# Retention stage: scores in one pass over four PSUM banks, and a chunk's work spread over one more period

## The reference, cut to what matters

```
x = x + retention(layernorm(x))          # 8 sequences of 512 rows, 256 columns, 16 heads of 16
Q, K = rotate(xn @ WQ), rotate(xn @ WK)  # position rotation
V = xn @ WV
D[h,i,j] = gamma_h ** (i-j) for i >= j, else 0
R = einsum(einsum(Q, K) * D, V)          # per head
R = group_norm(R) * gamma + beta         # over the 16 columns of a head
y = R @ WO
```

## Time and profile before

| what | value |
|---|---|
| three runs | 2053.95, 2053.84, 2051.27 us; median 2053.84 |
| the profiled execution | 2054.74 us, its span 2053.0 us |
| mean granted TensorE clock | 0.92 of full speed |
| PE busy | 1724.3 us, 84% of the span |
| PE weight loads | 1280.7 us, 62% |
| DVE, ACT, POOL busy | 1209.3 us (59%), 667.7 us (33%), 583.1 us (28%) |
| first and last transpose of XN in retention | 1438.0 and 1753.5 us from the span's start |

### The profile page before, as it was taken

How to read it: one execution, slowest core, us unless ns; L and a number is a source line. 1 busy time by engine, 2 the same in 40 slices (tenths; PEclk the granted TensorE clock), 3 DMA queues, 4 the chain that set the end, 5 groups by cost and what they waited for, 6 DMA issues and landing times. The chain is left out here.

```text
span 2053.0 us, 33292 instructions
## 1 busy us (share of the span) xinstructions
PE 1724.3 (84%) x10092; PEld 1280.7 (62%) x10092; DVE 1209.3 (59%) x3206; ACT 667.7 (33%) x2056; POOL 583.1 (28%) x668
## 2 busy tenths in 40 slices
PE   4767766999899967267857999996899999799998
PEld 2444435777677744156756888885566666456655
DVE  5999994777677765799843221222677777422221
ACT  2545554554455424012320111111344444211111
POOL 2434432000000011787516333332344443200000
PEclk9998987999999989678865999998999999799999
DMA  6000000000000000000022324222000000000000
GB/s 184 19 13 15 15 18 11 11 11 12 13 11 12 1 9 0 6 3 21 34 95 67 93 85 110 92 86 98 27 27 26 26 26 26 1 11 20 10 20 21
DMA packets 55111, 71.08 MB, mean 35 GB/s; under 512 B 7074, under 2 KB 44898, under 8 KB 54626
## 3 DMA queue, kind: packets, MB, share of 16 engines
q1 hardware_dynamic: 37218, 40.46, 6.3%
q0 software_dynamic: 6912, 18.88, 3.6%
q10 hardware_dynamic: 10880, 10.49, 1.5%
HBM read 46.61 MB, written 23.20 MB: 34 GB/s over the span
## 5 line engine op out<-in xcount | busy, mean ns | idle before, releaser
L801 ACT ACTIVATE probs<-psS,nm 128x256 f32<-128x256 f32 x256 | 118.9, 469 | 189.5 <-DVE nm L834 189.5
L409 PE MATMUL psKV<-wkv,XT 128*128 128x512 f32 x256 | 135.8, 679 | 52.2 <-DVE acc L545 32.5
L1576 DVE COPY YE<-e_psY 128x512 f32<-128x512 f32 x40 | 27.7, 691 | 220.6 <-PE e_psY L1522 220.6
L545 DVE SCALAR_TENSOR_TENSOR acc<-psKV,G,acc 128x128 f32<-128x128 f32 x544 | 150.2, 333 | 6.7 <-ACT gated L470 6.7
L1512 PE MATMUL e_psH<-e_XT,w 128*128 128x256 f32 x640 | 147.1, 384 | 0.0
L1522 PE MATMUL e_psY<-w,e_HT 128*128 128x256 f32 x640 | 144.0, 379 | 0.0
L832 DVE TENSOR_REDUCE mx<-psS 128x2 f32<-128x512 f32 x128 | 87.9, 686 | 90.9 <-PE psS L722 90.9
L722 PE MATMUL psS<-Rec,QT 128*128 128x256 f32 (+1 forms) x512 | 133.7, 384 | 5.4 <-issue 4.5
L1482 POOL DMA_INDIRECT XE<-token_rows,held x80 | 76.0, 950 | 200.2 <-PE e_psX L1499 180.5
L1522 PEld LDWEIGHTS e_psY<-w,e_HT 128*128 128x128 f32 x640 | 121.6, 190 | 16.5
L1512 PEld LDWEIGHTS e_psH<-e_XT,w 128*128 128x128 f32 x640 | 120.6, 193 | 15.4
(11 more groups left out here) (254 smaller groups left out, 3872.0 us busy)
## 6 DMA issues: line engine op xcount, KB each, us to landing
expert_out<-YE ACTq DMA_DIRECT2D x40, 256.0 KB, 2.2
w<-in_w SPq DMA_DIRECT2D x16, 512.0 KB, 4.3
X<-in_x SPq DMA_DIRECT2D x8, 512.0 KB, 7.6
x_turned<-XT SPq DMA_DIRECT2D x32, 128.0 KB, 2.1
XS<-x_turned SPq DMA_DIRECT2D x8, 512.0 KB, 4.0
token_rows<-o_XN SPq DMA_DIRECT2D x32, 128.0 KB, 1.7
out_x<-X SPq DMA_DIRECT2D x8, 512.0 KB, 2.9
QT<-in_sel SPq DMA_DIRECT2D x2, 1024.0 KB, 11.5
```

What stands on the lines that cost most here:

```text
L409: mm = pe.matmul(psKV[v % 2][half][:, :, :], XT[:, v, c, :], wkv[:, c, half * 512:(half + 1) * 512], start=(c == 0), stop=(c == KC - 1))
L545: ins = nc.vector.scalar_tensor_tensor(acc[:, v % 2, e, :], kv, g, acc[:, v % 2, e, :], ALU.mult, ALU.add)
L801: nc.scalar.activation(probs[:, b.q % 4, hg, :], psS[b.q % 2][:, hg, :], ACT.Exp, bias=nm[:, b.q % 2, hg:hg + 1], scale=scale, accum_out=s ...
```

## The change

It changes which bank holds what, how many periods a chunk passes through, and the order in every engine's list.

**Banks.** `psS` becomes four banks, one for each 32-row group, and `scores` issues all 16 products in one pass that goes round the four groups. To make room, turned x and the V product share one bank (`psXV`; the output product goes to its V half as before), R, the new state and the turned inverses share one (`psRS`), and the variances go into the first columns of `psQK`. The sharing adds waits: `project_v` waits for the next chunk's `xt_evac` (turned x read by ACT), `inverses_turned` for `st_done` (the new state read by DVE), `to_state` for `r_read` (R read by ACT), `variances` for `rot_done` (psQK read by DVE).

**Periods.** A chunk now passes through four periods after its preparation: new (0), one (-1), two (-2), three (-3). Rows are added and their statistics taken two periods ahead (before: one), normalised and turned one period ahead, gathered three ahead. Scores are made at -1; masked half at -1 and half at -2; R, its squares, variances and inverses at -2; the inverses turned, the result and the output at -3. Keys are copied at 0 and queries at -1 (XT, QT doubled, Kr four deep).

**Copies.** `values` copies V from PSUM once; the split by even and odd heads, `values_parted`, reads that copy in SBUF one period later.

```diff
-        psT = k.ps(ctx, "n_psT", [P, 2, KC, P])
+        psXV = k.ps(ctx, "n_psXV", [P, 2, D])
         psQK = k.ps(ctx, "n_psQK", [P, 2 * D])
-        psV = k.ps(ctx, "n_psV", [P, 2 * D])[:, 0:D]
         psK = k.ps(ctx, "n_psK", [P, 2, KC, P])
-        psX = k.ps(ctx, "n_psX", [P, 2, KC, P])
-        psVar, psInv = psX[:, 0, 0, 0:H1], psX[:, 1, :, :]
-        psS = [k.ps(ctx, f"n_psS{s}", [P, KC, 2, P]) for s in range(2)]
-        psR = k.ps(ctx, "n_psR", [P, 2, KC, P])[:, 0, :, :]
+        psRS = k.ps(ctx, "n_psRS", [P, 2, KC, P])
+        psS = [k.ps(ctx, f"n_psS{r}", [P, KC, 2, P]) for r in range(4)]
+        psX, psV = psXV[:, 0, :].rearrange("p (c t) -> p c t", c=KC), psXV[:, 1, :]
+        psR, psNew = psRS[:, 0, :, :], psRS[:, 1, :, :]
+        psInv, psVar = psR, psQK[:, 0:H1]
...
+            def project_v(c):
+                pe.wait_ge(xt_evac, upto(c.g + 2))
+                pe.wait_ge(z_added, c.g + 1)
...
+            def scores(c):
+                pe.wait_ge(x_evac, c.g * 2 + 4)
+                pe.wait_ge(s_masked, c.g * 4 + 4)
+                for h in range(KC):
                     for par in range(2):
                         for r in range(4):
...
+            def to_state(c):
+                pe.wait_ge(r_read, c.g + 2)
...
+            def variances(c):
+                pe.wait_ge(sq_ready, c.g + 1)
+                pe.wait_ge(rot_done, upto(c.g + 3) + 1)
...
+            def inverses_turned(c):
+                pe.wait_ge(inv_spread, c.g + 1)
+                pe.wait_ge(st_done, c.g + 3)
...
+            def deviation(c):
+                act.wait_ge(stat_ready, c.g + 1)
+                act.wait_ge(xn_ready, c.g + 1)
```

More of the change, by code:

```diff
@@ L1702, in peeled @@
                 step(g // TS, g % TS, lambda d: 0 <= g + d < NT)
-            for g in range(-2, TS):
+            for g in range(-3, TS):
                 peeled(g)
@@ L1755, in scores @@
[L1755 to L1778, removed]
+            def turn_x(c):
+                pe.wait_ge(xn_ready, c.g + 1 + 2)
+                pe.wait_ge(z_added, c.g)
+                pe.wait_ge(v_evac, c.g)
+                for h in range(KC):
+                    mm = pe.transpose(psX[:, h, :], XN[:, c.x, h * P:(h + 1) * P], k.ident[:, :])
+                mm.then_inc(xt_ready, 1)
@@ new lines, in scores, with from_state, from_chunk @@
+                mm.then_inc(s_ready, 1)
+            def from_state(c):
+                pe.wait_ge(st_done, c.g + 2)
+                for h in range(KC):
+                    pe.matmul(psR[:, h, :], state[:, h, :], QT[:, c.x, h, :], start=(h == 0), stop=False,
+                              skip_group_check=True)
+            def from_chunk(c):
+                pe.wait_ge(s_masked, c.g * 4 + 4 + 4)
+                pe.wait_ge(vpar_ready, c.g + 1)
+                for h in range(KC):
+                    for par in range(2):
+                        for r in range(4):
+                            n = (h * 4 + r) * 2
+                            mm = pe.matmul(psR[32 * r:32 * r + 32, h, :], Vpar[par][:, c.x, n * DH:(n + 2) * DH],
+                                           ST[:, r, h, par, :], start=False, stop=(r == 3 and h == 1 and par == 1),
@@ L1801, in inverses_turned @@
[L1801 to L1805, removed]
-                mm.then_inc(inv_ready, 1)
[L1808 to L1813, removed]
+            def to_state(c):
+                pe.wait_ge(r_read, c.g + 2)
+                for h in range(KC):
+                    mm = pe.matmul(psNew[:, h, :], Kr[:, c.s, h * P:(h + 1) * P], V[:, c.x, h * P:(h + 1) * P],
+                                   start=(h == 0), stop=(h == KC - 1), skip_group_check=True)
+                mm.then_inc(st_ready, 1)
@@ L1814, in out @@
+            def out(c):
+                pe.wait_ge(rt_ready, c.g + 1 + 1)
+                pe.wait_ge(v_evac, upto(c.g + 3) + 1)
+                for h in range(KC):
+                    mm = pe.matmul(psV[:, :], RT[:, h, :], wo[:, h, :], start=(h == 0), stop=(h == KC - 1))
                 mm.then_inc(z_ready, 1)
             def step(i, s, has):
-                g, entering, attending, leaving = i * TS + s, has(0), has(-1), has(-2)
-                if attending:
-                    scores(g - 1, 0)
@@ L1820, in step @@
[L1820 to L1841, removed]
+                new, one, two, three = Chunk(i, s, 0), Chunk(i, s, -1), Chunk(i, s, -2), Chunk(i, s, -3)
+                if has(-3):
+                    inverses_turned(three)
+                if has(0):
+                    project_qk(new)
+                if has(-3):
+                    out(three)
@@ L1843, in _ @@
+                if has(-2):
+                    from_state(two)
+                    from_chunk(two)
+                if has(-1):
+                    scores(one)
+                if has(-2):
+                    if not two.ends:
+                        to_state(two)
+                    variances(two)
+                if has(1):
+                    turn_x(Chunk(i, s, 1))
+                if has(0):
+                    turn_qk(new)
+                    project_v(new)
             stream(pe, step)
@@ L2065, in step @@
             def step(i, s, has):
[L2066 to L2087 removed]
+                new, one, two, three = Chunk(i, s, 0), Chunk(i, s, -1), Chunk(i, s, -2), Chunk(i, s, -3)
+                if has(-2):
+                    mask(two, 2)
+                if has(-3):
+                    result(three)
+                if has(-2):
+                    mask(two, 3)
+                if has(0):
+                    rotate(new)
+                if has(2):
+                    arrived(Chunk(i, s, 2), 0)
+                if has(-3):
+                    add(three)
+                if has(2):
+                    arrived(Chunk(i, s, 2), 1)
+                if has(1):
+                    norm(Chunk(i, s, 1))
+                if has(2):
+                    statistics(Chunk(i, s, 2))
+                if has(-1):
+                    mask(one, 0)
+                    mask(one, 1)
+                if has(-2):
+                    inverses(two)
+                    carry_on(two)
             stream(dve, step)
```

326 lines of the change are left out of this document (151 added, 175 removed).

## The result

The changed kernel takes **2094.77 us** (median of four runs, 2093.66 to 2095.70) against 2053.86 us for the kernel before on the same chip: a ratio of **1.0202, 95% interval 1.0184 to 1.0220**, some 41 us slower. The forecast was 2083 us, a ratio of 1.014; the range held the time.

A forecast was written before the change was run, and what follows sets the result against it. PE, busy 39.46 of 41 us, was taken to bound the kernel at 10.14 us a period. Profiled 2054.74 + 4.5 (loop and ends) + 25 (clock) = 2084, the runs' median 0.9 lower: 2083 us, range 2053 to 2125.

The forecast's parts named there:

- The direction: Whole kernel: slower was given a chance of 0.82, same 0.09 and faster 0.09.
- the bound of 8.7 us: Middle of retention: if PE alone set the pace, the period would fall from 10.14 to 8.7 us.
- The pass of 1.1 us: Scores on PE: two groups of 1.16 us become one pass, taken as 1.1 us.
- The upper bound of 2.1: Scores on PE: without more overlap than now, the one pass would take 2.1 us.
- The loop of 10.3 us: QK to next QK through DVE's statistics, deviation, read of R and project_v: 10.3 us against 10.14, +4 us over 27 periods.
- The ends: First periods -4 us, first chunk's XN +1, last full period -2, drain +5.5; together +0.5 us.
- The clock: Middle: PE's light stretches drop it to 1.2 GHz, +2.9 us per period hit, 0.3 of 29 periods: +25 us.
- the light stretch: Part of each period where PE idles 1.6 us, then does state, variances and small transposes; a third of the period.
- low clock in most periods: Rival: over half of the middle's periods hit by the low clock, 2110 to 2145 us; chance 0.13.
- the first case: Main forecast: loop closed and clock lost in some periods, 2066 to 2110 us; chance 0.57.
- What would show it: Trace signs: R read 1.5 to 2 us after from_chunk, drain 29 to 32 us; wrong if QK to QK under 9.
- The faster rival: DVE's statistics come early enough for ACT, so PE's 8.7 us set the period: 2012 us; chance 0.09.

The follow-up runs named there:

- e1: Changed kernel with ACT's read of R moved ahead of the root of the statistics (deviation): 2016.05 us, ratio 0.9822 to the kernel before.
- e9: Changed kernel with ACT's read of R, variances' root and turned-x copy ahead of deviation, and DVE's second mask behind inverses and new state: 2009.19 us.
- e3: Changed kernel with an extra unread PE product of 2 x 384 columns behind the scores: 2062.55 us, ratio 1.0051 to the kernel before.
- e7: e3 with one more ACT copy of 128x256 directly ahead of the read of R: 2075.70 us, ratio 1.0115 to the kernel before.
- e6: Changed kernel with one unread PE pass of 384 columns behind the scores, the first of e3's two: 2068.07 us, ratio 1.0071 to the kernel before.
- e4: Changed kernel with the scores in two passes, each over two of the four banks: 2092.39 us, ratio 1.0192 to the kernel before.

## Why the prediction was right

**The direction: right; the bound of 8.7 us: near, but by luck.** PE at 8.7 us a period was named as what the change would reach but for the loop; e1, with the loop open, has 8.80. But PE's own work there is 38.68 / 41 x 8.80 = 8.3 us, 0.4 less than the sum, and short waits make up the 8.80; e9, with 8.45, lies under the bound that was named. The change took 1.5 us from PE's period and not 1.1: besides the scores the QK product went from 1.98 to 1.88 us.

**The pass of 1.1 us: right**, 1.17. The upper bound of 2.1 was too high, since two passes back to back take 1.72.

**The loop of 10.3 us: right.** The periods at full clock are 10.30, with 10.56 and, in e3, 10.45 for two of each four, and e7 shows that 0.30 us put into the path comes out as 0.31. As a term it was +4; with the clock kept (e3) the 29 periods are 29 x 10.34 - 294.12 = +5.8 us.

**The ends: nearly right.** Forecast -4, +1, -2 and +5.5. From the first to the third QK product -2.3 us stand against -3, the last period is 8.21 us, 2.1 under the 10.3 of the loop, against -2, and the drain is +4.6 against +5.5. Loop and ends together were +4.5 by the sum, and are +10 by the ratio of e3; a part of these 10 lies in e3's own last period and drain, which the extra product lengthens (9.50 us and 30.9 against 8.21 and 29.85).

**The clock: right in kind, and the term that was mis-sized.** This is the step "the light stretch is a third of the period, and I take 0.3 of 29: +25 us". In place of 8.7 periods at +2.9 us the trace has 19 periods over 10.6 us. Against e3's 10.34, the twelve longest (12.47 to 13.00) are 29.8 us longer in all, 2.5 each, and the other seven (11.13 to 11.84) 7.4 us, 1.1 each. In all that is 37 us in the trace, and 31 us by the ratios of e3 and of the changed kernel. So a fully hit period cost a little less than the +2.9, and far more periods were hit than I took. The share of the period in which PE does little was no measure of the share of periods hit. The rival "low clock in most periods" had the better count, with 19 of 29, but priced each at the full +2.9; its lower end, 2110, is 15 us above the result. So the place in the first case's interval, 2066 to 2110, is in part luck: the count was too low by half, the price a little too high, and the loop with the ends, +4.5 against +10, was too low as well. All in all the sum came out 12 us under the measured time.

The Trainium skill ("TensorE: Matmul & The Clock Gate", section "Why this matters for your kernels") ties the loss to idle gaps between bursts longer than any here: PE's longest wait in the middle was 2.6 us. By that rule the time would have been 2059; the trace disagrees, with clocks of 0.83 to 0.92 in the windows of the middle. Another section of the page, "A second HAM failure mode: psum-queue depth-cycling", tells of a kernel whose clock went to and fro because PE was briefly idle between groups often; the rows of the changed kernel agree with that, and that section was the one to use.

**What would show it.** R read right behind `deviation`, 2.5 us after from_chunk and not 1.5 to 2; project_v 0.06 us behind the copy of turned x; PE's waits before to_state and variances; drain of 29.85 in 29 to 32: all seen. QK to QK under 9 us came only in the second and the last period (8.29 and 8.21), which the loop doesn't hold.

**The faster rival** needed the statistics early. e1 came within 5 us of its 2012 us by another way: the statistics end as late as before, 6.6 us behind QK's start for 6.4, but no longer hold the read.

**Open.** What decides in which periods the clock falls was not settled: the pattern repeats with the sequences of four chunks, which are also where the longest waits are, but no run varied the one without the other. The length of the wait does not decide it alone. In the changed kernel the 1.77 us wait that ends at 1557.29 is followed by a QK product of 3.03 us and the 1.88 us wait that ends at 1582.31 by one of 1.88; in e6 three of the six waits of 1.8 us between 1490 and 1720 have a drop behind them, and in e7 one of two equal waits of 1.44 us, as shown.

## What to carry to other kernels

When a step is moved within one engine's list, ask of every instruction behind it whose result it now waits for through the queue, and follow that round to itself: the sum of the durations on the way round is a floor for the period that no saving elsewhere lowers. A hole in TensorE's work can cost twice, as here, once as idle time and once as clock, so a saving of PE work that only widens a hole may bring nothing (e4) or make a kernel slower, as the changed kernel is slower than e3; filling the hole with useless work is a cheap test of how much of a loss is clock. And what a saving on an engine is worth is only known together with the order around it: measure it again once the next wait is gone.

## What the runs showed of the hardware that was not expected

Adding 1.56 us of TensorE work to each period made the kernel 31 us faster, as the granted clock of the middle, between 0.83 and 0.92 in the windows, went to 1.00. In the changed kernel, with a wait of 1.8 to 2.6 us in nearly every period, 19 of 29 periods were slow; in e4, with waits of 1.2 to 2.1, 18; in e6, with waits of 0.9 to 1.8, seven; in e7, with waits of up to 1.4, the clock fell once, and in e3, with waits of up to 1.1, not at all. These runs also differ in PE's work, so they give no length of wait by itself. Thirty-two score records over two row groups at a time take 1.72 us back to back, where 16 of them alone take 1.16, and 1.17 over four groups.
